# Moving the digit extraction of a top-16 gather from VectorE to ScalarE and TensorE

## The chip, the cores and the metric

One NeuronCore of a Trainium2 chip runs the whole program. The metric is device time in microseconds; the kernel before takes 2163.54 us (median of 3 runs, 2162.77 to 2164.7). Lower is better.

## What is computed

The input is 32 audio clips of 40000 samples. Each is cut into 313 frames of 128 samples, which a DCT turns into rows of 128. Then come attention of the rows with themselves (scores, softmax, sum) and, per row, a product-key expert layer. All else is cut here to that layer:

```
q   = layernorm64(hid @ Wq.T + bq)            # 8 heads x 64, two halves of 32
s0  = l2norm(q0) . l2norm(keys0)              # 64 scores per half
ix0, ix1 = the 16 best of each half
cs  = s0[i] + s1[j];  ci = ix0[i] + ix1[j]    # 256 cells per head
fs, pos = top_k(cs, 16);  fi = ci[pos]        # an index between 0 and 126
out += sum over 8 heads, 16 picks of softmax(fs) * gelu(hid . down[fi]) * up[fi]
```

The index `fi` is a sum of two indices below 64, so only 127 of the experts can be met.

## The kernel before, in words

Two clips make a pair of 626 rows, cut into 5 tiles of 128 rows (the last overlaps); 16 pairs give 80 tiles. Each engine has its own queue, written out in order by `drive`: for each pair k, tile slot t (0 to 4) and phase p (0 to 3) first `slot(k, t, p)` (the expert layer), then `front(k + 1, t, p)` (DCT, attention and norms of the pair after). Pairs 1 to 13 run in a hardware loop (`Fori`). With n = 5k + t, one slot of one engine works on several tiles at once: scores of tile n + 1, top-16 of tile n, cells of tile n - 1, weights of tile n - 2 ... Engines meet by counting semaphores only; an engine that waits holds back all that stands behind in its own queue.

The part around the change belongs to tile n - 3, whose 128 rows have 16 picks in each of 8 heads. GpSimd has made `Ye` (L877, L879), the index minus 1.5 of every picked cell. At the end of phase 3 of the slot before, TensorE turns it (L492, `rows`) into the PSUM tile `STE` (semaphore `eb_full`): 4 heads x 32 places on the partitions, 2 groups of heads x 128 rows in the 256 columns. The index is split as 4 * hi + y: `alpha` is a 0/1 mask over the 32 high digits (L1052, eight comparisons of 128x1024 against `hi`, which holds the high digit and three copies shifted by 32, 64 and 96), `beta` one over the four low digits (L1058, four comparisons against `lo`). Before the change VectorE makes `hi` and `lo` itself in phase 1: L1038 rounds to a multiple of four by adding and subtracting a large constant, L1043 makes the three shifted copies, L1045 subtracts to get `lo`.

What follows: GpSimd multiplies `beta` with the three bf16 parts of the weights (`wp`, L680, L708 and L711 on ScalarE, with `less` on TensorE, L498, between them) to `bw` (L887); TensorE contracts `alpha` and `bw` in four groups of quads, one per phase (L531); ScalarE copies each group to `WD` (L725); GpSimd sums it (L845 to L850) and ScalarE spreads it into `Gd` (L686).

Other names in the prediction: L671, L673, L675 make zexp, m and wexp at the head of ScalarE's phase 0, behind VectorE's last match of the 54 cells (`c2`); L692 turns indices to numbers (`idxf`), and GpSimd adds them to cells `ci` (L832), for which it also waits for `beta`. Of the front: at (2, 1) VectorE gives the seed of the second row norm (L905) and GpSimd refines it (L755); P is the query projection (L440) with its squares (L653), VAR the variances (L449, L450), taken by VectorE in `v` (L981) at (3, 3); at (4, 0) TensorE transposes the standard deviations and ScalarE copies `hidT` (L658) and `stdT` (L661, L663), for which the next scores (L483) wait; at (-1, 3), in the queue behind slot (k, 4, 3), lie the transposes and DCT of the pair after the next. The Gelu (L695) stands in slot t = 4, phase 0.

## Time and profile before

| | |
|---|---|
| median of 3 runs | 2163.54 us |
| the profiled execution | 2162.05 us, its span 2160.3 us |
| VectorE (DVE) busy | 2009.1 us, 93%, 16198 instructions |
| TensorE (PE) busy | 1695.4 us, 78% |
| GpSimd (POOL) busy | 1578.2 us, 73% |
| ScalarE (ACT) busy | 1108.3 us, 51%, 3515 instructions |
| TensorE's granted clock, mean | 0.724 of full speed |

Busy times are of one profiled execution. An engine's busy share says how long it executed, not how long others waited for it. Idle time in square brackets behind a row is that of the engine just before the row, with what ended it. A row with xN stands for N like instructions in a row, and its time runs from the start of the first to the end of the last.

### The profile page before, as it was taken

The numbers are of one execution on the slowest core, as the hardware profiler recorded it, in microseconds if no ns is written. First come the engines' busy times: TensorE is split into PE (matmuls) and PEld (weight loads), VectorE is DVE, ScalarE is ACT, GpSimd is POOL, SyncE is SP. The second block draws the span as 40 slices with busy tenths as digits, with TensorE's granted clock in tenths as the row PEclk, the third lists the DMA queues.
The fourth block names the chain that finished last, engine by engine and source line by source line (L and its number), as shares of the span: only waits on it lengthen the run. The fifth ranks groups of instructions, "written<-read, shape, count | busy, mean of one in ns | idle before, by whom it ended". The sixth has DMA issues, their size and how long they took to land.

```text
span 2160.3 us, 51105 instructions
## 1 busy us (share of the span) xinstructions
PE 1695.4 (78%) x10975; PEld 1326.3 (61%) x10975; DVE 2009.1 (93%) x16198; ACT 1108.3 (51%) x3515; POOL 1578.2 (73%) x3519
## 2 busy tenths in 40 slices
PE   5566798877879787787887889778777988878666
PEld 3345585756757565575666657566565767667555
DVE  3299999999999999999999999999999999999993
ACT  3334555465554546554455555545555454654343
POOL 2247787777778867777877777777777877878775
PEclk9676777678667867777777577767767676776655
DMA  1000000000000000000000000000000000000000
GB/s 34 12 9 4 16 9 11 11 5 17 5 17 5 9 14 8 17 5 17 5 5 17 8 17 5 17 5 5 17 8 15 8 11 11 6 12 9 6 6 10
DMA packets 46583, 23.56 MB, mean 11 GB/s; under 512 B 4955, under 2 KB 46116, under 8 KB 46390
## 3 DMA queue, kind: packets, MB, share of 16 engines
q1 hardware_dynamic: 46390, 21.80, 3.6%
q14 instruction: 171, 1.40, 0.2%
q8 instruction: 22, 0.36, 0.1%
HBM read 11.52 MB, written 10.26 MB: 10 GB/s over the span
## 4 chain that ended last, share of the span: by engine, by line
DVE 62%; PE 17%; POOL 11%; issue 7%; ACT 2%; SPq 0%; another core or an unknown queue 0%; DVEq 0%; DMA 0%; POOLq 0%; ACTq 0%
DVE hrest L1022 9%; DVE alpha L1052 8%; DVE idx L1028 7%; DVE idx L1031 7%; DVE vals L1019 6%; PE FB L449 5%; DVE vals L1026 5%; POOL bw L887 4%; PE QB L531 3%; DVE crest L1082 3%; DVE c L1088 3%; PE FB L440 3%; DVE top L1085 2%; DVE beta L1058 2%; DVE top L1079 2%
## 5 line engine op out<-in xcount | busy, mean ns | idle before, releaser
L531 PE MATMUL QB<-bw,alpha 128*128 128x48 bf16 x5120 | 554.2, 277 | 73.0 <-POOL bw L887 42.0
L531 PEld LDWEIGHTS QB<-bw,alpha 128*128 128x128 bf16 x5120 | 521.1, 151 | 111.5 <-issue 95.3
L887 POOL TENSOR_TENSOR bw<-beta,wp 128x1024 bf16<-128x1024 bf16 x240 | 503.7, 2128 | 11.6 <-ACT wp L711 11.5
L725 ACT ACTIVATE WD<-QB 32x96 f32<-32x96 f32 x1280 | 307.1, 240 | 92.4 <-PE QB L531 81.0
L832 POOL TENSOR_TENSOR ci<-idxf 128x64 f32<-128x64 f32 (+3 forms) x400 | 123.9, 343 | 201.4 <-DVE beta L1058 201.0
L1052 DVE TENSOR_SCALAR alpha<-hi 128x1024 bf16<-128x1024 bf16 x640 | 270.6, 494 | 0.0
L483 PE MATMUL SC<-WK,hidT 128*128 128x512 f32 x320 | 225.5, 794 | 42.8 <-ACT stdT L663 38.4
L1031 DVE FIND_INDEX8 idx<-vals,hrest 128x8 uint32<-128x64 f32 x1280 | 250.6, 220 | 0.0
L1028 DVE FIND_INDEX8 idx<-vals,sraw 128x8 uint32<-128x64 f32 x1280 | 250.6, 219 | 0.0
L1022 DVE MATCH_REPLACE8 hrest<-vals,sraw 128x64 f32<-128x64 f32 x1280 | 250.0, 209 | 0.0
L1019 DVE MAX8 vals<-sraw 128x8 f32<-128x64 f32 x1280 | 169.2, 209 | 0.0
L1026 DVE MAX8 vals<-hrest 128x8 f32<-128x64 f32 x1280 | 167.4, 209 | 0.0
L718 ACT ACTIVATE ofin<-QB 128x128 f32<-128x128 f32 x80 | 22.2, 277 | 282.0 <-PE QB L531 278.9
L755 POOL TENSOR_TENSOR sa<-sy 128x6 f32<-128x6 f32 x96 | 19.6, 205 | 194.1 <-DVE sy L905 189.1
L832 POOL TENSOR_TENSOR cs<-vs 128x64 f32<-128x64 f32 (+3 forms) x400 | 136.9, 375 | 7.3 <-POOL vs L857 2.1
L440 PE MATMUL FB<-hidTn,WcT 128*128 128x313 f32 x256 | 122.3, 640 | 18.4 <-ACT hidTn L648 10.8
L449 PE MATMUL FB<-indc,sq 128*128 128x24 f32 x640 | 134.2, 358 | 0.7 <-ACT sq L653 0.7
L483 PEld LDWEIGHTS SC<-WK,hidT 128*128 128x128 f32 x320 | 72.4, 246 | 100.0 <-issue 91.2
L519 PE MATMUL QB<-upR,Gd 128*128 128x128 f32 x640 | 127.2, 363 | 4.5 <-issue 4.2
L449 PEld LDWEIGHTS FB<-indc,sq 128*128 128x128 f32 x640 | 129.7, 299 | 1.1 <-ACT sq L653 1.1
L492 PE MATMUL U<-ident,Yw 128*128 128x128 f32 x640 | 127.0, 362 | 0.0
L705 ACT ACTIVATE sraw<-SC 128x1024 f32<-128x1024 f32 x80 | 83.0, 1038 | 81.1 <-PE SC L484 80.2
(206 smaller groups left out, 4085.2 us busy)
## 6 DMA issues: line engine op xcount, KB each, us to landing
res<-h_scratch SPq DMA_DIRECT2D x80, 64.0 KB, 1.8
xin<-in_x SPq DMA_DIRECT2D x32, 128.0 KB
h_scratch<-h2n SPq DMA_DIRECT2D x32, 128.0 KB
out<-ofin SPq DMA_DIRECT2D x64, 64.0 KB, 1.6
h_scratch<-h2n SPq DMA_DIRECT2D x32, 28.5 KB
out<-ofin SPq DMA_DIRECT2D x16, 57.0 KB
xin<-in_x SPq DMA_DIRECT2D x32, 28.0 KB
xin<-in_x SPq DMA_DIRECT2D x32, 0.2 KB
```

Source lines behind the costliest of these rows:

```text
L449: mm(bank[:, 40 * tt:40 * tt + 24], sq[:, c, cols], indc[:, c, :], start=(c == 0), stop=(c == 3))
L483: mm(SC[:, cols], hidT[:, START[t1]:START[t1] + 128], WK[:, cols], start=True, stop=False)
L531: last = mm(bank[:, 48 * u:48 * u + 48], alpha[:, buf, a, :, 8 * p + u], bwv[:, :, a, :, 8 * p + u], start=(a == 0), stop=(a == 1))
L725: last = A(WD[r, RING[(t - 4) % NT], :, 8 * p:8 * p + 8], blocks[r, :, :, g], ACT.Copy)
L832: last = tt(o, a0, a1, ALU.add)
L887: last = tt(bw[:, buf, NY * i:NY * i + NY, :], beta[:, buf, :, :], wp[:, buf, i, :].unsqueeze(1).to_broadcast([128, NY, 256]), ALU.mult)
L1019: V.max(vals[:, buf, i, 0:8], raw[i]).then_inc(chain, 1)
L1022: V.match_replace(rest[i], vals[:, buf, i, 0:8], raw[i], -1e30).then_inc(chain, 1)
L1026: V.max(vals[:, buf, i, 8:16], rest[i]).then_inc(chain, 1)
L1028: V.max_index(idx[:, buf, i, 0:8], vals[:, buf, i, 0:8], raw[i]).then_inc(chain, 1)
L1031: last = V.max_index(idx[:, buf, i, 8:16], vals[:, buf, i, 8:16], rest[i])
L1052: last = V.tensor_scalar(a8[:, :, :, xx, :], h8, float(NY * xx), None, ALU.is_equal)
```

## The change

ScalarE makes all four versions of the high digit from PSUM at the head of phase 0. It adds a bias of 768 - 32c and writes bf16; between 512 and 1024 neighbouring bf16 numbers are four apart, so the store rounds to a multiple of four. The digits so carry an offset of 768, which the comparisons for `alpha` add too. TensorE then subtracts the high digit (with the offset) from `STE` in PSUM at the head of phase 1, ahead of the scores, and ScalarE reads the rest with a bias of 768 as the low digit, at the head of its phase 1. The three groups of VectorE instructions go; its comparisons stay.

```diff
-ROUND4 = 1.5 * 2.0 ** 25
+BASE = 768.0
@@ tensor: slot
+                if p == 1 and exists(k, t, 3):
+                    pe.wait_ge(s["his_full"], n - 2)
+                    mm(STE, minusb[:], hi[:, 0, :], start=False, stop=True, skip_group_check=True).then_inc(s["lo_psum"], 1)
                 if p == 1 and exists(k, t, -1):
                     k1, t1 = (k, t + 1) if t < NT - 1 else (k + 1, 0)
                     scores(k1, t1)
@@ scalar: slot
+                if p == 0 and exists(k, t, 3):
+                    act.wait_ge(s["eb_full"], n - 2)
+                    after(act, s["alpha_full"], n - 3)
+                    for c in range(NS):
+                        last = A(hi[:, c, :], STE, ACT.Identity, bias=cdig[:, c:c + 1])
+                    last.then_inc(s["his_full"], 1)
                 if p == 0 and exists(k, t, 2):
...
+                if p == 1 and exists(k, t, 3):
+                    act.wait_ge(s["lo_psum"], n - 2)
+                    after(act, s["beta_full"], n - 3)
+                    A(lo[:], STE, ACT.Identity, bias=cdig[:, 0:1]).then_inc(s["lo_full"], 1)
                 if p == 1 and exists(k, t, 5):
@@ gpsimd: setup
+                for c in range(NS):
+                    nc.gpsimd.memset(cdig[:, c:c + 1], BASE - float(NY * NX // NS * c))
@@ vector: slot
-                    if digits:
-                        dve.wait_ge(s["eb_full"], n - 2)
-                        V.tensor_scalar(hi[:, 0, :], STE, ROUND4, ROUND4, ALU.add, ALU.subtract
-                                        ).then_inc(s["hi_full"], 1)
-                    if digits:
-                        dve.wait_ge(s["hi_full"], n - 2)
-                        for c in range(1, NS):
-                            last = V.tensor_scalar(hi[:, c, :], hi[:, 0, :], float(NY * NX // NS * c), None, ALU.subtract)
-                        last.then_inc(s["his_full"], 1)
-                        V.tensor_tensor(lo[:], STE, hi[:, 0, :], ALU.subtract).then_inc(s["lo_full"], 1)
                     if digits:
                         dve.wait_ge(s["his_full"], n - 2)
...
-                            last = V.tensor_scalar(a8[:, :, :, xx, :], h8, float(NY * xx), None, ALU.is_equal)
+                            last = V.tensor_scalar(a8[:, :, :, xx, :], h8, BASE + float(NY * xx), None, ALU.is_equal)
```

Besides, the turned `Ye` no longer closes its accumulation group in PSUM (`rows` loses its argument `end`), since the subtraction now does.

## Rows read from the trace of the kernel before

**Rows 1.** The page: busy us (share of the span) xinstructions of each engine.
```profile
PE 1695.4 (78%) x10975; PEld 1326.3 (61%) x10975; DVE 2009.1 (93%) x16198; ACT 1108.3 (51%) x3515; POOL 1578.2 (73%) x3519
```
**Rows 2.** The waits of VectorE: us in total, times, longest us.
```profile
DVE v L981 <- PE FB L450: 29.9, 13, 21.5
```
**Rows 3.** The timeline from S to V: start us, us, instruction, idle before.
```profile
1024.36 0.20 POOL L755 TENSOR_TENSOR sa<-sy 128x6 f32<-128x6 f32 x1 [9.32 <-DVE sy L905]
...
1040.51 1.77 PE L531 MATMUL QB<-bw,alpha 128*128 128x48 bf16 x16 [1.39 <-POOL bw L887]
...
1061.75 0.20 DVE L981 TENSOR_SCALAR v<-FB 128x40 f32<-128x40 f32 x1 [0.99 <-PE FB L450]
```
**Rows 4.** Groups by line on VectorE: xcount, busy us, mean ns of one, idle before.
```profile
L1043 DVE TENSOR_SCALAR hi<-hi 128x256 bf16<-128x256 bf16 x240 | 62.9, 317 | 2.8
...
L1038 DVE TENSOR_SCALAR hi<-EB 128x256 bf16<-128x256 f32 x80 | 33.2, 414 | 8.2 <-PE EB L492 8.2
L1045 DVE TENSOR_TENSOR lo<-EB,hi 128x256 bf16<-128x256 f32 x80 | 33.1, 414 | 0.0
```
**Rows 5.** Timeline of VectorE, a slot t = 2.
```profile
1019.04 0.41 DVE L1038 TENSOR_SCALAR hi<-EB 128x256 bf16<-128x256 f32 x1
...
1020.23 2.77 DVE L1052 TENSOR_SCALAR alpha<-hi 128x1024 bf16<-128x1024 bf16 x8
```
**Rows 6.** Timeline of ScalarE, slot t = 3 of pair A.
```profile
1040.59 0.38 ACT L680 ACTIVATE wp<-U 128x256 bf16<-128x256 f32 x1
1040.87 0.52 ACT L692 ACTIVATE idxf<-idx,cquart 128x256 f32<-128x256 uint32 x1
1042.39 1.00 ACT L725 ACTIVATE WD<-QB 32x96 f32<-32x96 f32 x4 [1.00 <-PE QB L531]
```
**Rows 7.** Timeline of ScalarE: two copies, and two Exp with a bias, of 313 columns.
```profile
1030.81 0.76 ACT L648 ACTIVATE hidTn<-FB 128x313 f32<-128x313 f32 x2
...
1119.36 0.93 ACT L628 ACTIVATE E<-FB,cneg 128x313 f32<-128x313 f32 x2
```
**Rows 8.** Timeline of ScalarE, slot t = 3 ahead of pair B.
```profile
658.87 1.00 ACT L725 ACTIVATE WD<-QB 32x96 f32<-32x96 f32 x4 [0.35 <-PE QB L531]
```
**Rows 9.** Timeline of ScalarE and VectorE, slot t = 4 of pair A.
```profile
1073.13 0.26 ACT L663 ACTIVATE stdT<-FB 81x128 bf16<-81x128 f32 x1
...
1073.10 1.39 DVE L1058 TENSOR_SCALAR beta<-lo 128x256 bf16<-128x256 bf16 x4
1074.41 0.27 DVE L1066 TENSOR_REDUCE zs<-zexp 128x8 f32<-128x128 f32 x1
```
**Rows 10.** Timeline of ScalarE and VectorE, slot t = 4 of pair B.
```profile
688.08 1.00 ACT L725 ACTIVATE WD<-QB 32x96 f32<-32x96 f32 x4 [1.02 <-PE QB L531]
...
690.35 0.26 ACT L663 ACTIVATE stdT<-FB 81x128 bf16<-81x128 f32 x1
...
689.19 1.39 DVE L1058 TENSOR_SCALAR beta<-lo 128x256 bf16<-128x256 bf16 x4
```
**Rows 11.** Timeline of TensorE (scores), ScalarE and VectorE, to slot t = 0 behind pair A.
```profile
1073.74 2.05 PE L483 MATMUL SC<-WK,hidT 128*128 128x512 f32 x2 [3.49 <-ACT stdT L663]
...
1096.84 0.98 ACT L725 ACTIVATE WD<-QB 32x96 f32<-32x96 f32 x4
...
1099.18 0.62 DVE L1058 TENSOR_SCALAR beta<-lo 128x256 bf16<-128x256 bf16 x4
```
**Rows 12.** Timeline of ScalarE and VectorE, slot t = 0 behind pair B.
```profile
710.64 1.00 ACT L725 ACTIVATE WD<-QB 32x96 f32<-32x96 f32 x4
...
715.27 0.63 DVE L1058 TENSOR_SCALAR beta<-lo 128x256 bf16<-128x256 bf16 x4
```
**Rows 13.** Timeline of ScalarE and VectorE, slot t = 1 behind pair B.
```profile
738.46 0.52 ACT L628 ACTIVATE E<-FB,cneg 57x313 f32<-57x313 f32 x1 [0.41 <-PE FB L421]
...
741.83 0.73 DVE L1058 TENSOR_SCALAR beta<-lo 128x256 bf16<-128x256 bf16 x4
```
**Rows 14.** Timeline of GpSimd near the end, without a front.
```profile
2058.72 1.55 POOL L832 TENSOR_TENSOR ci<-idxf 128x128 f32<-128x128 f32 x5 [6.60 <-DVE beta L1058]
```

More of the change, by code:

```diff
@@ L101, in build @@
         cquart = sb("cquart", [128, 1])
+        cdig = sb("cdig", [128, NS])
         c15 = sb("c15", [128, 80])
@@ L238, in build @@
             rn_steps halves_full vs_full cs_full idxf_full ci_full c2_full zexp_full m_full wexp_full zs_full
-            rz_full wz_full y_full st_full w1_full rest1_full w2_full rest2_full w3_full hi_full his_full lo_full
+            rz_full wz_full y_full st_full w1_full rest1_full w2_full rest2_full w3_full his_full lo_psum lo_full
             beta_full alpha_full bw_full quads_full wd_full ws_steps g_full gd_full fo_full fin_full
@@ L485, in scores, with rows @@
                 last.then_inc(s["scores_full"], 1)
-            def rows(src, eye, dst, end):
+            def rows(src, eye, dst):
                 for a in range(2):
@@ L492, in rows @@
                         last = mm(dst[:, 128 * a:128 * a + 128], cells, eye[:], start=(a == 0 and blk == 0),
-                                  stop=(end and a == 1 and blk == 1), skip_group_check=True)
+                                  stop=False, skip_group_check=True)
                 return last
@@ L536, in slot @@
                     pe.wait_ge(s["y_full"], n - 1)
-                    rows(Ye, identb, STE, True).then_inc(s["eb_full"], 1)
+                    rows(Ye, identb, STE).then_inc(s["eb_full"], 1)
                     after(pe, s["w3_full"], n - 2)
-                    rows(Yw, ident, U[:, 0:256], False).then_inc(s["st_full"], 1)
+                    rows(Yw, ident, U[:, 0:256]).then_inc(s["st_full"], 1)
             def late(t, p):
```

## The prediction

> **What bounds the kernel now.** I read the page's busy line first: VectorE 2009.1 of 2160.3 us, TensorE 1695.4, GpSimd 1578.2, ScalarE 1108.3 [rows 1]. Then the waits: VectorE's largest in the loop is for the variances (L981, 29.9 us in 13 waits, one of them 21.5 in the start) [rows 2]. So VectorE never rests for long, and a first reading is that each of its instructions costs its length. Then I followed one pair of clips in time, because a short wait that returns every period can mean a second chain of nearly the same length. It does. VectorE gives the seed of the second row norm just before 1024.36; GpSimd, idle for 9.32 us, starts on it there and goes on to the index cells, Yw, Ye and the bw product; TensorE waits 1.39 us for bw, starts its quads at 1040.51 and is never idle until the variances are in PSUM; VectorE, 0.99 us early, takes them at 1061.75 [rows 3]. Call the seed S and that last moment V. From S to V (37.4 us of some 127.8 a pair) the chain GpSimd-ScalarE-TensorE sets the time; from V to the next S (90.4 us) VectorE does. Twelve of the fourteen V's behind the first two show such a wait, 0.55 to 1.09 us; the other two, at 1188.67 and 1571.17, show none.
>
> **What VectorE loses.** Five instructions per tile go, 33.2 + 62.9 + 33.1 us busy [rows 4], 129 in all. That sum is too high: the last one overlaps the first alpha. From the start of L1038 to the start of the first alpha comparison it is 1020.23 - 1019.04 = 1.19 us [rows 5]. In other slots it is 1.36 to 1.66, where an L1043 stands still beside GpSimd; I take it that this stall passes to the first alpha, so 1.2 us per tile (bounds 1.2 and 1.6), 96 us in 80 tiles if VectorE set every microsecond.
>
> **What ScalarE gains.** Per tile four high digits at the head of phase 0 and one low digit at the head of phase 1, each 128x256 from PSUM to bf16 with a bias read from memory. That form isn't in the trace. The nearest: the copy of the same shape (L680) is followed after 1040.87 - 1040.59 = 0.28 us [rows 6]. What the bias adds: two Exp of 313 columns with it take 0.93 us for both, 0.52 the length of one, so the pace is 0.41; two copies of 313 columns take 0.76 with 0.43, pace 0.33 [rows 7]. So 0.28 + 0.08 to 0.09, or 0.37 a piece (bounds 0.28, as the copy, and 0.50, the whole length of the Identity at L692), 1.47 us for four; length of one 0.47. A handover from engine to engine is 0.07 us, a low digit can be read 0.54 us after its start. ScalarE has the room on average (1108.3 + 80 x 5 x 0.37 = 1256 us). What counts is where it has none, since its queue is in order: everything behind the four pieces comes 1.47 us later, except what it waits for anyway. The Trainium skill (ScalarE: Activation LUTs, What ACT_TABLE_LOAD costs) gives 280 ns + 0.833 ns a column with a pointer bias and an overlap of 93 ns, which makes an estimate of 0.40 a piece and 1.60 for four; the rows above agree on what the bias adds. By it each of the three delays below would be 0.13 longer, and the total some 4 us.
>
> **What TensorE gains.** One 256-column bf16 subtraction per tile at the head of phase 1, before the scores; a neighbour of that form (L498) sets the next one back by 0.11 us at the high clock and 0.22 at the low. In its queue it waits for the high digits, and the scores stand behind it.
>
> **The four places of a pair**, worked for two pairs, A (V = 1061.75) and B (V = 677.82).
>
> *S to V, slot t = 3.* ScalarE's queue: idxf, then WD, which waits for the quads, then the squares of P, for which TensorE's next projections wait. In A idxf ends at 1041.39 and WD starts at 1042.39: of 1.47 us 1.00 is hidden, 0.47 is left [rows 6]. In B idxf ends at 658.52, WD starts at 658.87: 1.12 is left [rows 8]. With the subtraction (0.11): V comes 0.6 us (A) or 1.2 us (B) later. VectorE's own gain in this slot is worth nothing; its low digit comes about 1 us later than now, and it still reaches V first.
>
> *V to beta, slot t = 4.* ScalarE works without a break here through the Gelu, hidT and stdT, and only then comes the low digit. stdT ends at 1073.39; 1.47 later is 1074.86, and the low digit is ready at 1075.40. VectorE starts beta at 1073.10 now and would be there at about 1071.9; it has to wait some 3.5 us and starts 2.3 later than now. GpSimd then stands before the ci cells, which wait for beta, so the four betas take 0.54 rather than the present 1.31 (1074.41 - 1073.10) and 0.77 comes back: net +1.5 us [rows 9]. In B ScalarE already waits 1.02 in front of WD; stdT goes from 690.61 to 691.06, ready at 691.60 against 689.19: +2.4 - 0.8 = +1.6 [rows 10].
>
> *Slot t = 0.* TensorE's scores at 1073.74 wait for stdT, and from there it has no gap up to the next scores at 1093.86; the transposes and DCT of the next pair, whose results ScalarE copies, move with stdT. Behind them come the four high digits, a table load, zexp, m, wexp, wp, idxf, WD, and then the low digit. WD ends at 1097.82 in A: + 1.47 + 1.47 + 0.54 = 1101.3, and VectorE, now at 1099.18, would be there at 1099.18 + 1.5 - 1.2 = 1099.5: it starts 2.1 later than now [rows 11]. In B WD ends at 711.64: + 0.45 + 1.47 + 0.54 = 714.1, VectorE comes at 715.27 + 1.6 - 1.2 = 715.7, no wait, +0.4 [rows 12].
>
> *Slots t = 1 and 2.* The next norm's seed is given right after this beta, so all moves with it. In t = 1 the last Exp before the low digit ends 2.85 us ahead of beta in B (738.98 and 741.83): + 1.47 + 0.54 leaves it 0.36 behind VectorE; in A the same two are 4.5 us apart, enough [rows 13]. Gains 1.2 in A, 0.8 in B. In t = 2 ScalarE waits for c2 before and has 4.3 us spare behind: 1.2 in both.
>
> Sum of a pair: A +2.1 - 1.2 - 1.2 + 0.6 = +0.3; B +0.4 - 0.8 - 1.2 + 1.2 = -0.4. Four of the loop's pairs have B's times within 0.2 us, two have A's (V = 1061.75 and 1698.93), the rest lie between: I take -0.1.
>
> **The sum.** 13 periods from S to S at -0.1: -1.3. The start up to the first such S: five slots in which ScalarE has room, -6.0. The last S to V: +1.2. The end: +1.6 in its slot t = 4, then six slots without a front, where GpSimd waits 6.60 us for beta and ScalarE is long done with WD [rows 14], -7.2; three chains of the drain through w2 are longer by the low digit, 0.4 each, +1.2. Together -10.5 us (-1.3 - 6.0 + 1.2 + 1.6 - 7.2 + 1.2). The profiled execution took 2162.05 (span 2160.3 and 1.75 around it), which gives 2151.6; it lies 1.5 under the median of the three runs, 2163.54, so I predict 2153 us.
>
> **Rivals.**
> *VectorE sets all* (2067 us): -96 us. For it: the 93% of row 1. The Trainium skill says so too: its Perfetto Trace Analysis page (Identifying the Most-Contended Engine) takes occupancy on VectorE as the measure of what to shorten first. Against it: the waits at V. It needs the low digit never late and the V chain not longer. Chance 0.06.
> *Only V's chain binds* (2102): the low digits are in time, four slots gain 1.2 and V costs 1.0: -3.8 x 13 = -49, with -12 outside, -61. For it: ScalarE's pieces may run at the copy's 0.28, or the table-load and Gelu slots have room that I don't see. Against it: rows 9, where 2.2 us would have to vanish. Chance 0.14.
> *The order of the queues loses* (2190): at t = 0 TensorE stands at the subtraction until the high digits are there, 1.5 us, with the scores behind. If the pieces take 0.50 and the pairs fall into A's timing, t = 4 costs 2.2, t = 0 brings that to 3.0, t = 1 and 2 give 0.6 + 1.2 back, V's chain costs 1.5: +2.7 a pair, 35 us, less 9 outside. It decides where the low digit at t = 0 comes more than 1.5 us behind VectorE in most pairs; in A it does, by 1.8. Chance 0.24.
> *Gain and loss cancel outright* (2163): a per-pair sum of +0.7 in place of -0.1. Chance 0.16.
> That the edit doesn't do what it says I hold for negligible: types and shapes of alpha and beta stay, only the constants of the comparison change.
>
> **Chances.** My forecast 0.40, its own range 2142 to 2162. A measurement tells 0.2% (4.3 us). Faster: 0.36 of the forecast, 0.14, 0.06: 0.56. Same: 0.04 + 0.16 = 0.20. Slower 0.24. The range leaves out the first rival, some of the second and the tail of the third: 2112 to 2178.
>
> **What would show it.** Right: a wait of VectorE at beta in each slot t = 4, some 3.5 us, and in part of t = 0, by ScalarE's low digit; VectorE's busy time about 115 to 130 us down with its idle time up by about as much; the wait at V grown from 0.6 to 1 us to 2 or more; high digits with a pace near 0.37. Wrong: no wait at beta in t = 4 (then the second rival), a period above 128 us (the third), or waits at alpha for the high digits, which I put at none but 0.4 us in t = 4.

## The result, and the profile after

The changed kernel takes 2169.8 us (median of 20 runs, 2162.3 to 2177.3), the kernel before 2163.5 (20 runs, 2160.6 to 2166.0). The ratio is 1.0028, with a 95% interval of 1.0018 to 1.0038: slower by 0.28%, where I had forecast 0.5% faster. All numbers read from a trace below are of one profiled execution. The profiled execution took 2171.7 us, 2169.9 of it span.

The page of the kernel after, busy time by engine, answers to [rows 1]; the second line is its chain that ended last, which was 62% VectorE before:

```profile
PE 1743.0 (80%) x11055; PEld 1346.1 (62%) x11055; DVE 1892.9 (87%) x15798; ACT 1249.4 (58%) x3915; POOL 1634.1 (75%) x3523
PE 42%; ACT 18%; POOL 17%; DVE 12%; issue 11%; SPq 0%; ACTq 0%; POOLq 0%; DMA 0%; DVEq 0%; another core or an unknown queue 0%
```

VectorE was relieved of 116 us and the time grew by 6: what it was spared came back as waiting. Its waits in the kernel after (us in total, times, longest) show where, and answer to [rows 2]:

```profile
DVE beta L1064 <- ACT lo L694: 106.8, 65, 3.5
DVE alpha L1058 <- ACT hi L675: 29.4, 19, 9.0
DVE v L997 <- PE FB L451: 27.0, 8, 21.6
```

65 of the 80 tiles wait at beta for ScalarE's low digit. I had expected that of the slots t = 4 and part of t = 0, some 20 to 25 tiles. The groups of the digit lines and of GpSimd's product (line, out<-in, count, busy us, mean ns, idle before) answer to [rows 4] and price the new instructions; `<-issue` stands for time in which the engine waited for nothing that the profile shows:

```profile
L675 ACT ACTIVATE hi<-EB,cdig 128x256 bf16<-128x256 f32 x320 | 125.2, 473 | 39.7 <-PE EB L493 21.7 <-issue 16.9
L694 ACT ACTIVATE lo<-EB,cdig 128x256 bf16<-128x256 f32 x80 | 37.5, 469 | 0.9
L507 PE MATMUL EB<-hi,minusb 128*128 128x256 bf16 x80 | 26.1, 326 | 36.6 <-ACT hi L675 36.6
L903 POOL TENSOR_TENSOR bw<-beta,wp 128x1024 bf16<-128x1024 bf16 x240 | 504.1, 2131 | 47.6 <-ACT wp L725 47.3
L1058 DVE TENSOR_SCALAR alpha<-hi 128x1024 bf16<-128x1024 bf16 x640 | 269.1, 491 | 29.5 <-ACT hi L675 29.4
```

TensorE stands 36.6 us before its subtractions, and GpSimd's wait for wp, which was 11.5 us in all before, is 47.3.

One line of the two pages shows something that the prediction did not reckon with, the packets by which instructions are brought in (packets, MB, share of the DMA engines' time), before and after:

```profile
q14 instruction: 171, 1.40, 0.2%
q14 instruction: 232, 1.89, 0.3%
```

Below, "ScalarE's late start" is what goes with them: in 12 of the loop's 13 pairs ScalarE's first instruction of slot t = 0, the first slot of the hardware loop's body, starts 1.2 to 1.6 us after ScalarE's last one and waits for nothing that the profile shows (the 16.9 us behind `<-issue` above). Before the change this row has no such time in it. ScalarE's first instruction there is now a high digit, whose input has been in PSUM for 6.8 to 9.9 us.

Mean length of a slot in us (from one zs to the next; the loop's 13 pairs), with what I had predicted for pairs A and B:

```
slot            before   after   change   predicted A / B   wait at beta / alpha, after
t = 3           23.87    24.43   +0.56                      2.05 / -
t = 4           26.72    27.82   +1.10                      2.55 / 0.82
t = 3 and 4     50.59    52.25   +1.66    +2.1 / +2.8
t = 0           26.31    26.94   +0.63    +0.6 / -1.2       1.21 / 0.43
t = 1           25.55    24.91   -0.64    -1.2 / -0.8       0.86 / -
t = 2           25.08    24.80   -0.28    -1.2 / -1.2       0.73 / -
a pair         127.53   128.90   +1.37    +0.3 / -0.4
```

### The profile page after: what moved, and what is told of

The parts are those of the page before. It is cut to its first block, busy times and chain, and to the rows that moved or that the text cites. A ratio compares the mean times of both kernels' runs of the same rounds, so it can differ in the third digit from the quotient of the medians.

```text
span 2169.9 us, 51440 instructions
## 1 busy us (share of the span) xinstructions
PE 1743.0 (80%) x11055; PEld 1346.1 (62%) x11055; DVE 1892.9 (87%) x15798; ACT 1249.4 (58%) x3915; POOL 1634.1 (75%) x3523
## 4 chain that ended last, share of the span: by engine, by line
PE 42%; ACT 18%; POOL 17%; DVE 12%; issue 11%; SPq 0%; ACTq 0%; POOLq 0%; DMA 0%; DVEq 0%; another core or an unknown queue 0%
PE QB L535 10%; PE FB L450 5%; PE SC L484 5%; POOL bw L903 4%; PE FB L441 3%; PE QB L523 3%; ACT hi L675 3%; PE FB L422 3%; ACT WD L739 3%; POOL sa L769 3%; PE FB L430 2%; PE U L493 2%; PE FB L398 2%; POOL Ye L895 2%; DVE idx L1044 2%
## 5 line engine op out<-in xcount | busy, mean ns | idle before, releaser
L903 POOL TENSOR_TENSOR bw<-beta,wp 128x1024 bf16<-128x1024 bf16 x240 | 504.1, 2131 | 47.6 <-ACT wp L725 47.3
L1058 DVE TENSOR_SCALAR alpha<-hi 128x1024 bf16<-128x1024 bf16 x640 | 269.1, 491 | 29.5 <-ACT hi L675 29.4
L484 PE MATMUL SC<-WK,hidT 128*128 128x512 f32 x320 | 247.0, 865 | 49.4 <-ACT stdT L667 47.3
L848 POOL TENSOR_TENSOR cs<-vs 128x64 f32<-128x64 f32 (+3 forms) x400 | 175.3, 472 | 7.3 <-POOL vs L873 2.1
L1064 DVE TENSOR_SCALAR beta<-lo 128x256 bf16<-128x256 bf16 x320 | 57.2, 238 | 107.5 <-ACT lo L694 106.8
L675 ACT ACTIVATE hi<-EB,cdig 128x256 bf16<-128x256 f32 x320 | 125.2, 473 | 39.7 <-PE EB L493 21.7
L484 PEld LDWEIGHTS SC<-WK,hidT 128*128 128x128 f32 x320 | 78.8, 271 | 111.1 <-issue 102.0
L523 PE MATMUL QB<-upR,Gd 128*128 128x128 f32 x640 | 131.7, 372 | 4.5 <-issue 4.2
```

The costliest lines, as they stand in the source:

```text
L484: mm(SC[:, cols], hidT[:, START[t1]:START[t1] + 128], WK[:, cols], start=True, stop=False)
L523: mm(FO, Gd[:, y, :], upR[:, y, :], start=(y == 0), stop=False)
L675: last = A(hi[:, c, :], STE, ACT.Identity, bias=cdig[:, c:c + 1])
L848: last = tt(o, a0, a1, ALU.add)
L903: last = tt(bw[:, buf, NY * i:NY * i + NY, :], beta[:, buf, :, :], wp[:, buf, i, :].unsqueeze(1).to_broadcast([128, NY, 256]), ALU.mult)
L1058: last = V.tensor_scalar(a8[:, :, :, xx, :], h8, BASE + float(NY * xx), None, ALU.is_equal)
```

## Experiments

Medians in us; "clock" is the median, over the executions, of TensorE's mean granted clock; "alpha long" counts the tiles, of 80, whose eight alpha comparisons took over 3.4 us from the first start to the last end (2.8 is their length when left alone).

```
kernel                                        time    ratio to before, 95%       clock   alpha long   idle at beta/alpha, digits
before                                        2163.5                             0.721   29           -
after                                         2169.8  1.0028 (1.0018 to 1.0038)  0.728   30           106.8 / 29.4
e1   no digits made, constant tiles read      2063.2  0.9526 (0.9504 to 0.9548)  0.737   28           -
e4   high digits on ScalarE, unread           2062.8  0.9530 (0.9512 to 0.9548)  0.762   26           -
e11  constant subtraction, low digit unread   2045.3  0.9454 (0.9437 to 0.9472)  0.751   26           -
e5   all digits made as in after, unread      2102.0  0.9699 (0.9663 to 0.9735)  0.731   32           -
e7   after, beta reads a constant tile        2124.1  0.9805 (0.9781 to 0.9830)  0.734   33           - / 43.2
e2   high on ScalarE, low on VectorE          2135.6  0.9864 (0.9849 to 0.9878)  0.718   31           27.0 (at lo)
e3   after, subtraction and low earlier       2205.4  1.0186 (1.0154 to 1.0217)  0.702   35           38.7 / 52.0
e6   high on VectorE, low as in after         2163.8  0.9998 (0.9984 to 1.0012)  0.728   31           13.6 / -
e8   ONE high digit on ScalarE, rest VectorE  2096.9  0.9679 (0.9663 to 0.9695)  0.725   2            20.4 (at hi)
e12  e8, lo before the copies                 2147.0  0.9925 (0.9911 to 0.9938)  0.726   31           13.2 (at lo)
e15  e8 with a second high digit on ScalarE   2122.3  0.9785 (0.9761 to 0.9809)  0.720   23           24.1 (at hi)
e14  e8's high digits, low as in after        2156.1  0.9956 (0.9943 to 0.9969)  0.734   31           39.4 (beta)
e9   before, one idle copy ahead of alpha     2178.7  1.0069 (1.0055 to 1.0083)  0.717   29           -
e10  before, lo before the copies             2171.0  1.0034 (1.0021 to 1.0048)  0.723   32           -
```

Not all of these differences belong to the edits alone. In after, e1, e3, e5, e7, e11 and e15 the executions of one and the same kernel differ by 11 to 30 us and go with the clock: some 8 to 19 us shorter for each 0.01 of mean granted clock (in before, e6, e9, e10 and e12 it is 3 us or less). e1 took 2056.2 us at a clock of 0.744 and 2071.1 at 0.731. Where two kernels were granted different clocks, the executions at like clocks are compared below as well. Which of the two is cause, the clock or the time, no run here shows.

### What the removal is worth, and what each step of the new way costs

**e1: no digits.** ScalarE's hi and lo, the subtraction and all waits for them are gone; hi and lo are constant tiles, so the digits are left out.

```
-  for c in range(NS): A(hi[:, c, :], STE, ACT.Identity, bias=cdig[:, c:c + 1])      # ScalarE
-  mm(STE, minusb[:], hi[:, 0, :], ...)                                              # TensorE
-  A(lo[:], STE, ACT.Identity, bias=cdig[:, 0:1])                                    # ScalarE
+  memset(hi[:], BASE); memset(lo[:], 0.5)                                           # once
```

> Leaves out the digits altogether: hi and lo are constant tiles, nobody reads STE (the output is not the reference's). It shows what VectorE's 1.2 us per tile are worth when nobody has to do the work. If VectorE sets the time everywhere: -96 us, 2067. My reading of before (the chain from S to V is as long as VectorE's work there, so one slot in five gives nothing): 4 x 1.2 x 13 and 12 at the ends, -74, 2090. If other chains catch VectorE in most slots: above 2115.

Measured 2063.2. Taking the five instructions off VectorE, and the wait for the turned indices with them, is worth 100 us: more than the 96 that I had set as the most it could bring at 1.2 us a tile. The mean stretch from S to V keeps its 37.0 us, and VectorE now waits at V 13 times behind the first pair, 1.6 to 2.9 us each, where it waited 0.55 to 1.1. So the chain to V does set its own stretch, and that slot gives nothing, as expected. The stretch from V to S falls from 90.5 to 83.8 us, by 1.7 a slot in four slots where I had 1.2: the value of a slot was set too low, and only so does the total come out near the rival that lets VectorE set every slot.

**e7: after, beta without its wait.** The low digit is made but beta reads a constant tile.

```
-  dve.wait_ge(s["lo_full"], n - 2)
-  last = V.tensor_scalar(beta[:, old, y, :], lo[:], y - 1.5, None, ALU.is_equal)
+  last = V.tensor_scalar(beta[:, old, y, :], loc[:], y - 1.5, None, ALU.is_equal)
```

> The changed kernel, but beta compares a constant tile, so VectorE never waits for the low digit, while ScalarE and TensorE still make it (output not the reference's). If the loss is VectorE's standing at beta: the 107 us of waits fall away and the time comes near 2105. If the lengthened queues of ScalarE and TensorE are the loss and VectorE's waits only their shadow: 2145 or more.

Measured 2124.1 (2102.7 to 2132.7; the trace is of the fastest): by the medians the wait at beta costs 46 us of the 107 between e1 and after, and at like clocks (0.728 to 0.731) 38 to 44. The other 60 or so are there although VectorE never waits for a low digit.

**e4: high digits on ScalarE, read by nobody** (e1, with the four ScalarE instructions put back).

```
   for c in range(NS): last = A(hi[:, c, :], STE, ACT.Identity, bias=cdig[:, c:c + 1])
-  h8 = hi[:].rearrange(...)
+  h8 = hic[:].rearrange(...)        # constant tile; no wait for his_full, no subtraction, no low digit
```

> After, with ScalarE's four high digits still made in phase 0 but read by nobody: VectorE compares constant tiles, there is no subtraction and no low digit. It is e1 (2063 us, no digits at all) plus 1.47 us of ScalarE per tile at the head of its phase 0. Theory 'lateness is carried' (what the added ScalarE time delays is passed on round the ring of TensorE, ScalarE and GpSimd, and VectorE meets it as waits elsewhere): 2090 us (2078 to 2105), with more waits at v L997 than the 51 us of e1. Rival 'only VectorE's waits for digits count': no wait for digits is left, so 2065 us (2060 to 2070).

Measured 2062.8, e1's time to 0.4 us, with 107 us more busy time on ScalarE. By the medians that costs nothing, as the rival named here says. But e4 was granted the higher clock (0.762 against 0.737); in the one pair of executions at like clocks it took 2070.3 us at 0.743 and e1 2056.2 at 0.744. So my theory that ScalarE's delay is carried round the ring is not borne out at the 27 us that it asked for, and a cost of up to some 14 us is not ruled out.

**e5: all digits made, none read** (e4, with subtraction and low digit).

```
+  pe.wait_ge(s["his_full"], n - 2)
+  mm(STE, minusb[:], hi[:, 0, :], start=False, stop=True)
+  act.wait_ge(s["lo_psum"], n - 2); A(lo[:], STE, ACT.Identity, bias=cdig[:, 0:1])
```

> After with all of its digit work in place (four high digits, subtraction on TensorE, low digit) and VectorE comparing constant tiles in both alpha and beta. It is e7 (2124 us) without the wait for the high digits. Theory 'lateness is carried': the subtraction at which TensorE stands adds to the delay, 2110 us (2095 to 2125), so that of after's 107 us above e1 some 45 are the queues' lengthening, some 15 the alpha wait and 45 the beta wait. Rival 'only VectorE's waits for digits count': 2065 us (2060 to 2072).

Measured 2102.0 (2088.7 to 2115.6): 39 us more than e4 by the medians and 18 to 27 between the executions nearest in clock (0.735 and 0.736 against 0.743), though VectorE waits for no digit. Here the rival falls and the first theory's number is met. VectorE's waits show where it surfaces:

```profile
DVE zs L1074 <- ACT zexp L683: 30.2, 10, 4.3
```

In e4 that wait is 0.1 us in all. zexp stands behind the high digits in ScalarE's queue in slot t = 0, and e5 has ScalarE's late start there (15.3 us in 11 pairs, 231 instruction packets), which e4 has not (171 packets). Of the 3.7 us by which a pair is longer in e5's trace than in e4's, 2.3 are in that slot.

**e11: a subtraction that does not stand.** As e5 without the high digits, the subtraction taking a constant tile and waiting for nothing.

```
-  pe.wait_ge(s["his_full"], n - 2)
-  mm(STE, minusb[:], hi[:, 0, :], start=False, stop=True)
+  mm(STE, minusb[:], hic[:, 0, :], start=False, stop=True)
```

> e5 without the four high digits on ScalarE and with a subtraction that takes a constant tile and waits for nothing; ScalarE's low digit stays behind it, unread, and VectorE compares constant tiles. e4 has shown that ScalarE's high digits alone cost nothing (2063 us). Theory 'TensorE's standing at the subtraction until ScalarE's high digits are there costs the 39 us of e5 above e4': 2064 us (2058 to 2070). Rival 'the subtraction's 0.2 us of TensorE and ScalarE's wait for it cost them': 2095 us (2085 to 2105).

Measured 2045.3, 57 us less than e5. So the instructions of the subtraction and of the low digit cost nothing by themselves. That this kernel is 18 us faster than even e1 goes with its clock: at 0.742 and 0.745 it took 2053.1 and 2052.1 us, e1 at 0.744 2056.2.

It is tempting to put the 39 us of e5 above e4 down to TensorE's stand at the subtraction, with the scores, less2 and the quads behind it (32.5 us in 14 stops in e5). The runs do not show that, since e11 takes away three things at once: the stand, the high digits and ScalarE's late start. The late start comes with exactly the four kernels in which ScalarE makes all five digits (after, e3, e5, e7: 3915 ScalarE instructions, 231 or 232 packets, 15 to 17 us of it); the other twelve, with 3835 or fewer, have 170 to 172 packets and none of it. It makes up about half of each stand too: in after's trace the 12 stands behind a late start last 2.65 to 3.05 us, the two without one 1.32 and 1.35. And e6, whose TensorE stands 181.0 us at the same subtraction in 41 stops, is not slower than before. The shares by the medians are then 39 us for stand and late start together, 22 for the wait at alpha (e7 less e5), 46 for the wait at beta (after less e7), 107 in all, against 100 from the removal; at like clocks around 0.735, e5 lies some 28 us above e1 and e7 some 31 above e5. A kernel with all five digits but without the late start was not run.

**e3: subtraction and low digit earlier.** The subtraction behind the quads of phase 0, the low digit behind phase 0's WD.

```
-  if p == 1: pe.wait_ge(s["his_full"], n - 2); mm(STE, minusb[:], hi[:, 0, :], ...)
+  if p == 0: (the same, behind the quads);  ScalarE's lo behind WD of p == 0
```

> The changed kernel with the subtraction behind the quads of phase 0 and the low digit directly behind WD of phase 0, ahead of the front's work of that phase (stdT, Exp, squares, h2n). If the low digit's place behind the front is the cause: the waits at beta fall from 2.5 to about 0.5 us in t = 4 and vanish in t = 1 and 2, time 2135 to 2145. If the total of ScalarE's added work or TensorE's stop at the subtraction is: 2162 or more, as the changed kernel.

Measured 2205.4: the wait at beta falls from 106.8 to 38.7 us as meant, and the kernel is 36 us slower. TensorE now stands earlier (30 stops, 41.2 us), the waits at v grow to 78.6 us and those at alpha to 52.0. The wait that was visible on VectorE was not the place to mend. TensorE's mean granted clock is 0.703 in this profile (0.728 in after), so part of the loss may be the clock's: at 0.718 it took 2190.2 us, after at 0.720 2172.3, 18 us apart instead of 36.

### Which share of the digits pays

**e2: high digits on ScalarE, low on VectorE.** No subtraction.

```
+  V.scalar_tensor_tensor(out=lo[:], in0=STE, scalar=BASE, in1=hi[:, 0, :], op0=ALU.add, op1=ALU.subtract)
```

> High digits by ScalarE as in the changed kernel, low digit by one VectorE instruction from PSUM (STE + 768 - hi, 0.41 us), no subtraction on TensorE. If the low digit's place at the end of the chain of queues is the cause: 0.8 us gained per slot in four of five, 0.8 lost at V, 2125 to 2135, no waits at beta, alpha waits as now or fewer. If the four high digits at the head of ScalarE's phase 0 are the cause: 2155 or more.

Measured 2135.6, faster than both kernels: 34 us under after with 48 us more on VectorE, and without the late start (171 packets).

**e6: the low digit alone moved** (before, with its lo replaced by the subtraction and a ScalarE copy).

```
-  V.tensor_tensor(lo[:], STE, hi[:, 0, :], ALU.subtract)
+  mm(STE, minusb[:], hi[:, 0, :], ...) on TensorE;  A(lo[:], STE, ACT.Copy) on ScalarE
```

> Before, with the low digit alone moved (subtraction on TensorE at the head of phase 1, ScalarE's copy of STE behind it); the high digits stay on VectorE. VectorE sheds only the 0.41 us of lo per tile (33 us). Theory 'the low digit's chain is what spoils the change': slower than before, 2180 us (2165 to 2195), since the four hi instructions of VectorE now come 1.4 us before the subtraction can start and beta follows alpha by only 3.4 us. Rival 'the low digit comes in time because alpha covers it': 2163 - 33 x 0.9 = 2135 us (2128 to 2145).

Measured 2163.8, no change (0.9984 to 1.0012): between both theories, an instruction of 33 us in all gone from VectorE (its busy time falls by 20) and nothing gained. TensorE's waits (us in total, times, longest) are worth a look:

```profile
PE EB L506 <- DVE hi L1050: 181.0, 41, 6.9
```

TensorE stands five times as long at the subtraction as in after, and the kernel is as fast as before, whose TensorE stood 102.5 us for ScalarE's `hid` (30.5 here) and 96.5 for GpSimd's `Ye` (39.6 here). What a stand costs depends on what stands behind it and on whether TensorE would have stood anyway.

**e8: one high digit on ScalarE.** The three shifted copies stay on VectorE (half a microsecond a tile), and so does the low digit.

```
+  A(hi[:, 0, :], STE, ACT.Identity, bias=cdig[:, 0:1])                                    # ScalarE
+  for c in range(1, NS): V.tensor_scalar(hi[:, c, :], hi[:, 0, :], 32.0 * c, None, ALU.subtract)
+  V.scalar_tensor_tensor(out=lo[:], in0=STE, scalar=BASE, in1=hi[:, 0, :], op0=ALU.add, op1=ALU.subtract)
```

> Only the first high digit on ScalarE (one instruction of 0.47 us per tile), the three shifted copies (63 us in all, 0.32 each at before's L1043) and the low digit (one scalar_tensor_tensor) on VectorE. Against e2 (2135.5 us) VectorE gets 63 us back and ScalarE is rid of 88 us. Theory 'lateness is carried, ScalarE's time counts as well as VectorE's': about even with e2, 2140 us (2130 to 2152). Rival 'VectorE's own time sets it': e2 plus 0.9 x 63 = 2190 us less the waits for digits that e2 has (27 us), so 2163 us (2155 to 2175).

Measured 2096.9, far below either theory: 3.2% faster than before, though only one instruction of 33 us in all has left VectorE, as in e6. VectorE's busy time nevertheless falls by 94.5 us, to 1914.6. Its groups say where the rest is. VectorE in e8:

```profile
L1055 DVE TENSOR_SCALAR alpha<-hi 128x1024 bf16<-128x1024 bf16 x640 | 229.8, 429 | 0.0
L1046 DVE TENSOR_SCALAR hi<-hi 128x256 bf16<-128x256 bf16 x240 | 53.8, 278 | 20.4 <-ACT hi L671 20.4
L1061 DVE TENSOR_SCALAR beta<-lo 128x256 bf16<-128x256 bf16 x320 | 50.1, 216 | 0.0
```

The alpha comparisons, untouched by the edit, take 229.8 us in place of 270.6 (before) or 269.1 (after), and beta 50.1 for before's 62.7. Eight alphas left alone take 2.8 us, and in before they take 4.1 to 4.6 in the loop's tiles of t = 1 and t = 4; in e8 two tiles are over 3.4 (12 more take 3.1 to 3.4). VectorE and GpSimd at t = 4 in before (start us, length us):

```profile
940.50 0.45 POOL L809 TENSOR_TENSOR stdin<-sdr,one 128x120 bf16<-128x120 f32 x1
940.76 4.23 DVE L1052 TENSOR_SCALAR alpha<-hi 128x1024 bf16<-128x1024 bf16 x8
940.90 0.52 POOL L817 TENSOR_TENSOR nB<-nB,std 128x80 f32<-128x80 f32 x1
941.39 0.50 POOL L818 TENSOR_TENSOR nC<-v,C 128x80 f32<-128x80 f32 x1
```

and the same place in e8:

```profile
908.07 3.67 POOL L811 TENSOR_TENSOR stdin<-sdr,one 128x120 bf16<-128x120 f32 x1
908.13 2.76 DVE L1055 TENSOR_SCALAR alpha<-hi 128x1024 bf16<-128x1024 bf16 x8
911.82 0.26 POOL L813 TENSOR_TENSOR sdr<-sdr,stdin 128x40 f32<-128x40 f32 x1
```

In before a GpSimd instruction is half done when alpha begins; from then on the two engines take turns: in each of before's 29 long tiles exactly 8 GpSimd instructions start during the 8 alphas, in the other 51 between none and 4. The alphas take 4.23 us here while GpSimd's instructions go on at 0.5 us. In e8 alpha begins as GpSimd's next instruction does, and that one stands until alpha is through: 3.67 us for one that takes 0.45 elsewhere. VectorE pays in the one case and GpSimd in the other, and here GpSimd can afford it.

**e12: e8 with lo ahead of the copies.** Same instructions, other order.

```
   V.scalar_tensor_tensor(out=lo[:], ...)      # now first
   for c in range(1, NS): V.tensor_scalar(hi[:, c, :], ...)
```

> e8 (2097 us) with lo computed before the three shifted copies; same instructions, other order. Theory 'phase beside GpSimd': e8 has alpha at 2.8 to 3.3 us in all five tiles of a pair, so there is little to win and up to 50 us to lose: 2095 to 2150, alpha's mean per instruction at or above e8's 429 ns. Rival 'VectorE's work sums': 2097 us (2093 to 2101).

Measured 2147.0: 50 us lost by order alone. e12 at t = 4:

```profile
932.77 0.83 POOL L811 TENSOR_TENSOR stdin<-sdr,one 128x120 bf16<-128x120 f32 x1
932.80 0.49 DVE L1048 TENSOR_SCALAR hi<-hi 128x256 bf16<-128x256 bf16 x3
933.42 3.99 DVE L1055 TENSOR_SCALAR alpha<-hi 128x1024 bf16<-128x1024 bf16 x8
```

The copies hold GpSimd's instruction up by 0.4 us, so that it is still running (to 933.60) when alpha begins at 933.42, and alpha takes turns again. Over the whole run alpha goes from 429 to 496 ns (+42 us busy) and beta from 216 to 274 (+18 us).

**e15: two high digits on ScalarE.**

```
-  A(hi[:, 0, :], STE, ACT.Identity, bias=cdig[:, 0:1])
+  for c in range(2): A(hi[:, c, :], STE, ACT.Identity, bias=cdig[:, c:c + 1])
```

> e8 (one high digit on ScalarE, 2097 us) with a second one there and two shifted copies left on VectorE; the low digit stays on VectorE, no subtraction. ScalarE's own time has been free (e4), VectorE sheds 0.16 to 0.2 us a tile and waits at most 0.37 us more where the indices are late (t=4). If alpha keeps clear of GpSimd's instructions as in e8: 2092 us (2082 to 2105). If it falls into step with them at t=1 and t=4 as in e2 and e12: 2140 us (2130 to 2150).

Measured 2122.3, between the two values: alpha is long in 14 of 16 tiles at t = 4 (3.95 us) and 9 of 16 at t = 1 (4.5), and below 3.4 elsewhere. Taking an instruction of 0.2 us a tile off VectorE made the kernel 25 us slower than e8 and its VectorE 28 us busier. One, two and four high digits on ScalarE give 2096.9, 2122.3 and 2135.6, in step with 2, 23 and 31 long alphas.

**e14: e8's high digits, after's low digit.** The subtraction waits for one ScalarE instruction instead of four.

```
-  pe.wait_ge(s["his_full"], n - 2)
+  pe.wait_ge(s["hi_full"], n - 2)             # one ScalarE instruction
```

> After with one high digit on ScalarE instead of four: the three shifted copies go back to VectorE (0.16 to 0.32 us each), the subtraction waits for one ScalarE instruction (0.47 us after the indices are there, not 1.57) and the low digit stays on ScalarE. If TensorE's stand at the subtraction and the late low digit are what spoils after, both shrink by 1.1 us a tile and VectorE takes on about 0.5 us: 2105 us (2085 to 2130), with beta's waits under 40 us in all. If instead any low digit by way of TensorE costs what after shows, its beta waits stay near 100 us: 2165 us (2150 to 2180). If alpha falls into step with GpSimd's instructions at t=1 and t=4 (over 4.2 us there), add 25 to 50 us to the first.

Measured 2156.1, at the upper end of the case with long alphas (31 of them). No wait for the high digit is left among TensorE's largest, the waits at beta fall from 106.8 to 39.4 us, as expected; but only 14 us of the time come back. The late start is gone too (172 packets), so the 14 us cannot be put down to the shorter stand alone, and 60 us more work on VectorE stand against them. Against e8, where the low digit stays on VectorE, it is still 59 us slower; it has 29 more long alphas, as many as e12, which is 50 slower than e8. That they are the cause here as well was not tested.

**e9 and e10: is it the phase alone?** Before with one idle instruction, and before with the order of e12.

```
e9:   V.tensor_tensor(lo[:], STE, hi[:, 0, :], ALU.subtract)
    + V.tensor_copy(idle[:], STE[:, 0:128])
e10:  V.tensor_tensor(lo[:], ...) moved ahead of the three copies
```

> Before, with one more VectorE instruction of about 0.2 us per tile between lo and alpha: a copy of 128 columns of STE (PSUM) into a tile that nobody reads. Theory 'phase beside GpSimd' (the eight alpha comparisons take 2.8 us when they begin in a gap between two GpSimd instructions and 4.2 to 4.9 us when one is in progress, which is the case in before at t=1 and t=4; what moves alpha by 0.2 us can change that): at t=4 alpha would begin 0.2 us later, about where GpSimd's instruction of before ends, so the 1.65 us would go there; +16 us of work less 16 x 1.65 = 26 us gives 2153 us (2125 to 2175), and the mean of alpha per instruction falls below 494 ns. Rival 'VectorE's work sums': 2164 + 16 x 0.9 = 2178 us (2174 to 2182), alpha's mean unchanged.

> Before, with the same instructions in another order: lo is computed before the three shifted copies, so that the copies and the eight comparisons of alpha follow each other without an instruction that reads PSUM between them. No work is added or taken. Theory 'phase beside GpSimd': which tiles' alpha runs at 2.8 and which at 4.2 to 4.9 us changes, and the time moves by more than 8 us to either side (2130 to 2155, or 2172 to 2185), with alpha's mean per instruction moving with it. Rival 'VectorE's work sums': 2164 us (2161 to 2167).

Measured 2178.7 and 2171.0; alpha's mean stays at 497 and 493 ns (494 before). The idle copy cost what the rival said, 15 us for 22 us of work, and moved no alpha out of step: I could not aim at the gap, since GpSimd's instructions there are of several lengths. e10 cost 8 us although alpha's mean stood still: the block from the first digit to zs is 0.22 us longer in t = 0 and in t = 2, probably because alpha now waits for the copy directly ahead of it; that was not tested. So the link between the length of alpha and the time rests on e8, e12 and e15.

## Why the prediction was wrong

**Steps that held.** Four high digits took 1.57 us from first start to last end, so a pace of 0.37 and 473 ns for one: as forecast. By the Trainium skill (ScalarE: Activation LUTs, What ACT_TABLE_LOAD costs) the estimate is 493 ns, from 280 ns + 0.833 ns a column; the trace has 473. At t = 4 all went as worked out; ScalarE and VectorE in the kernel after, answering to [rows 9]:

```profile
1206.76 0.26 ACT L667 ACTIVATE stdT<-FB 81x128 bf16<-81x128 f32 x1
1206.92 0.47 ACT L694 ACTIVATE lo<-EB,cdig 128x256 bf16<-128x256 f32 x1
...
1200.80 3.97 DVE L1058 TENSOR_SCALAR alpha<-hi 128x1024 bf16<-128x1024 bf16 x8 [0.52 <-ACT hi L675]
1207.49 0.81 DVE L1064 TENSOR_SCALAR beta<-lo 128x256 bf16<-128x256 bf16 x4 [2.72 <-ACT lo L694]
```

The low digit follows stdT at once and VectorE stands 2.72 us, with 0.52 at alpha: 3.2 of the 3.5 forecast. Slots t = 3 and 4 cost 1.7 us together where I had 2.1 to 2.8, so these two were if anything too dear. One sign of being right did not come: the wait at V did not grow to 2 us. The stretch from S to V grew by 0.4 us where I had 0.6 to 1.2, VectorE itself waits 2.05 us at beta in that slot, and at V it waits in 7 of the loop's pairs, 0.9 us at most.

**The step that failed: "Gains 1.2 in A, 0.8 in B. In t = 2 ... 1.2 in both".** Gained were 0.64 and 0.28, together 1.1 to 1.5 us less than forecast, which is about the whole miss of 1.5 us a pair. The forecast took over the positions of ScalarE and TensorE from the trace of before and moved only VectorE and the edited instructions ("ScalarE ... has 4.3 us spare behind"). What VectorE met there is on record: waits at beta of 0.86 us in t = 1 and 0.73 in t = 2, where I had put none. The first thing that the forecast left out is at t = 0, where TensorE now stands; ScalarE and TensorE in the kernel after, answering to [rows 11]:

```profile
1224.54 1.57 ACT L675 ACTIVATE hi<-EB,cdig 128x256 bf16<-128x256 f32 x4 [1.32 <-issue]
1226.17 0.39 PE L507 MATMUL EB<-hi,minusb 128*128 128x256 bf16 x1 [2.76 <-ACT hi L675]
1226.55 2.05 PE L484 MATMUL SC<-WK,hidT 128*128 128x512 f32 x2
```

I had priced that stand as part of a rival only, at 1.5 us. Where ScalarE starts on time it is 1.32 and 1.35, near that; in the 12 other pairs it is 2.65 to 3.05, since ScalarE's late start adds 1.2 to 1.6, a term that stands nowhere in the prediction. The same pair's t = 1 and t = 2, GpSimd, ScalarE and VectorE:

```profile
1269.49 0.38 ACT L725 ACTIVATE wp<-U 128x256 bf16<-128x256 f32 x1 [5.15 <-PE U L499]
1269.96 6.33 POOL L903 TENSOR_TENSOR bw<-beta,wp 128x1024 bf16<-128x1024 bf16 x3 [4.64 <-ACT wp L725]
...
1276.53 1.75 PE L535 MATMUL QB<-bw,alpha 128*128 128x48 bf16 x16 [1.62 <-POOL bw L903]
...
1281.19 1.86 ACT L640 ACTIVATE h2n<-h2c,hcs 128x128 f32<-128x128 f32 x6
1283.08 0.47 ACT L694 ACTIVATE lo<-EB,cdig 128x256 bf16<-128x256 f32 x1
...
1283.66 0.79 DVE L1064 TENSOR_SCALAR beta<-lo 128x256 bf16<-128x256 bf16 x4 [1.58 <-ACT lo L694]
```

Read from the top: ScalarE's 5.15 us of wait for less2 (the second `less`) are nothing new, they stand in before as well. New is when they end: this copy of wp starts 8.2 to 10.8 us after VectorE's last zs, against 4.4 to 6.7 in before. So GpSimd has waited 4.64 us before bw and TensorE 1.62 before the quads. ScalarE is then busy without a break from 1273.77 to 1283.05 (ofin, WD, the high digits, the exponentials, the row norms, h2n), and only then comes the low digit: 1.58 us of wait at a beta for which I had predicted none. The 4.3 us that ScalarE had to spare in the old trace are gone.

That the digits' place is late in t = 1 and 2 is read from the trace. What made it late is only in part shown. e5, where VectorE waits for no digit, says that the new path costs 18 to 39 us without those waits, and this is TensorE's stand, ScalarE's late start or both. But e2, which has no subtraction and no late start, has the same copy of wp at 8.2 to 10.8 us behind zs, and GpSimd waits 70.8 us for wp there. So the four high digits at the head of ScalarE's phase 0 bring this lateness about as well, and how it divides between them, the stand and the late start stays open.

**Slot t = 0** went on average as in A (+0.63), not as in B. This is near the third rival ("the pairs fall into A's timing", "TensorE stands at the subtraction"), but its numbers are not met: a period grew by 1.4 us and not by 2.7, the pieces took 0.37 and not 0.50, and the wait at beta was over 1.5 us in half of the pairs, 1.21 on average. The start gave 3.9 us instead of 6.0; its first t = 4 already waits 3.5 at beta. In the two traces the 13 periods from S to S made +17.6 us where -1.3 was predicted; start and end together made -7.9, where -9.2 was. The miss is in the loop.

**A term that was right by luck.** I took it that the shed instructions are worth 1.2 us each tile and their stall passes on to alpha. e1 gave 1.25 on average (100 us in 80 tiles), but as 1.7 in four slots of five and nothing in the fifth, and with alpha long in other slots than before. The length of alpha, which I had held constant at 494 ns, is a variable of 40 us busy (229.8 in e8, 269.1 in after): in after it happened to stay (30 long alphas for 29), and the sum escaped it. Had it moved as in e8, the forecast would have been off by more than its range.

**Occupancy as the measure.** The Trainium skill's rule that the most occupied engine is the one to shorten (Perfetto Trace Analysis, Identifying the Most-Contended Engine) names the right engine here, since e1 gains 100 us by relieving VectorE. It does not tell what a change is worth: VectorE's busy time fell by 116 us in after and the time rose by 6, by 20 us in e6 and the time stayed, by 94.5 in e8 and the time fell by 67.

## What to carry to other kernels

When work moves off the bound engine, ask of every engine that now waits on the new path what stands behind the wait in its queue, and let its lateness run on through the following slots: slack read from the old trace belongs to the old timing. The path that hands over once (e8: one ScalarE instruction, the rest where it was) brought 67 us, of which 50 are gone again when alpha is long (e12); the one that hands over three times, ScalarE-TensorE-ScalarE, cost 6. Compare the pages' instruction packets when instructions are added to a loop, and look at the clocks of the executions before a difference of 20 us is given a cause. And try small changes of order where two engines' work meets: e8 and e12 differ by 50 us and not by one instruction.

## What the runs showed of the hardware

**Two outcomes where VectorE's bf16 comparisons meet GpSimd.** The sixteen traces have 1280 tiles. In 413 no GpSimd instruction runs beside the eight alphas, and none of these is long (over 3.4 us). In 338 of the others the first alpha begins while a GpSimd instruction has been running for over 0.12 us and has over 0.1 us to go, and 263 of them are long; 65 of the 75 others began beside one of the additions that make the cells (`cs`), beside which only 2 of 67 were long. Of 85 that began between two GpSimd instructions 22 were long. With a start close to either end of a GpSimd instruction it falls both ways (164 of 444), and what decides then is open. The Trainium skill (SBUF — State Buffer, Who interferes with whom) describes the port pair of the two engines as an exclusive lock; the 3.67 us of a 0.45 us instruction in e8 agree with that, and so does the other outcome if the lock changes hands after each instruction, one GpSimd instruction for each alpha, as in before. Why GpSimd gets no turn in e8 and one after each alpha in before no run shows.

**A late start at the head of the loop's body.** With 3915 ScalarE instructions in a run, ScalarE's first instruction of slot t = 0 starts 1.2 to 1.6 us late in 11 or 12 of the loop's pairs and the run has some 60 instruction packets more; with 3835 or fewer neither is seen. In after's trace five such packets lie around each of these starts (1221.8 to 1225.0 us for the one at 1224.54), in e4's two. That the packets are ScalarE's instructions is likely and not shown.

**The same stand of TensorE costs differently.** 32.5 us of recorded stops go with 39 us of time in e5 against e4, together with the late start and a lower clock; 181.0 us in e6 go with none against before.
